# Self attention's output product on a two-layer Perceiver kernel: one full-precision product against three one-pass products of split operands

## The reference

```python
x = x + _L0_xattn_ref(_layernorm(x, axis=-1), ctx_512, ...)
x = x + _L0_attn_ref(_layernorm(x, axis=-1), ...)
x = x + _L0_ffn_ref(_layernorm(x, axis=-1), ...)
x = x + _L1_xattn_ref(_layernorm(x, axis=-1), ctx_512, ...)
x = x + _L1_attn_ref(_layernorm(x, axis=-1), ...)
x = x + _L1_ffn_ref(_layernorm(x, axis=-1), ...)
```

## Time and profile before

| | us |
|---|---|
| median of 3 runs | 2112.19 |
| lowest and highest of them | 2111.12, 2112.30 |
| span of the profiled execution, first to last instruction | 2106.8 |
| PE busy in it | 1996.1 (95%) |
| DVE, POOL, ACT busy | 1203.5 (57%), 972.1 (46%), 898.1 (43%) |
| L0a's first to last output product on PE | 440.4 to 532.6 |
| L1a's first to last output product on PE | 1462.3 to 1561.0 |

### The profile page before, as it was taken

The page is one execution under the profiler, slowest core; times in us unless marked ns, Lnnn a source line. Parts: engine busy times, 40 slices in busy tenths (PEclk is TensorE's granted clock), DMA queues, the critical chain, the costliest instruction groups (busy, mean ns, idle before and its releaser), DMA issues. The chain is left out here.

```text
span 2106.8 us, 28714 instructions
## 1 busy us (share of the span) xinstructions
PE 1996.1 (95%) x9018; PEld 1421.9 (67%) x9018; DVE 1203.5 (57%) x2739; ACT 898.1 (43%) x2115; POOL 972.1 (46%) x928
## 2 busy tenths in 40 slices
PE   7989999998999999999998999979978999999997
PEld 6868888776688744666656888767655555555553
DVE  4368998567551022555547899779863443444444
ACT  2356666334422100333335666635524444454542
POOL 1266684211352100676768666476203444555552
PEclk9999999999999999999999999989988999999999
DMA  5421221200311100111222121110345999989887
GB/s 209 150 100 42 58 58 37 82 1 1 120 42 52 35 1 0 52 57 61 70 107 66 43 67 43 66 67 1 110 148 154 312 298 327 210 213 221 209 218 186
DMA packets 103411, 226.29 MB, mean 107 GB/s; under 512 B 14288, under 2 KB 56784, under 8 KB 94768
## 3 DMA queue, kind: packets, MB, share of 16 engines
q1 hardware_dynamic: 80688, 170.85, 24.0%
q0 software_dynamic: 21136, 51.11, 11.9%
q10 hardware_dynamic: 1440, 2.49, 0.3%
HBM read 266.86 MB, written 42.48 MB: 147 GB/s over the span
## 5 line engine op out<-in xcount | busy, mean ns | idle before, releaser
L98 PE MATMUL banks<-L1f_w,L1f_xT 128*128 x760 | 265.1, 492 | 1.9 <-issue 1.3
L2872 POOL DMA_INDIRECT moe_sums<-L1f_y,L1f_row x94 | 149.3, 1589 | 219.5 <-DVE L1f_is_who L2739 162.2
L159 POOL TENSOR_TENSOR rstd<-rstd,power 128x1 f32<-128x1 f32 x48 | 35.4, 738 | 361.1 <-DVE rstd L153 361.1
L98 PEld LDWEIGHTS banks<-L1f_w,L1f_xT 128*128 128x128 f32 x760 | 138.0, 192 | 82.0 <-issue 6.8
L2690 DVE SCALAR_TENSOR_TENSOR L1f_z<-banks,L1f_share,L1f_sg 128x192 f32<-128x192 f32 x95 | 39.7, 418 | 147.8 <-ACT L1f_sg L2623 147.7
L2880 POOL DMA_INDIRECT L1f_xg<-moe_rows,L1f_row x95 | 94.2, 991 | 61.5 <-DVE L1f_spare L2730 24.6
L2623 ACT ACTIVATE L1f_sg<-banks 128x192 f32<-128x192 f32 x95 | 31.4, 331 | 206.9 <-PE banks L98 145.5
L98 PE MATMUL banks<-L0f_down,L0f_z 128*128 128x512 f32 x256 | 111.1, 592 | 1.5 <-DVE L0f_z L2147 1.5
L98 PE MATMUL banks<-L0f_hT_hi,L0f_ug_hi 128*128 128x512 f32 x256 | 100.0, 391 | 0.0
L98 PE MATMUL banks<-L0f_hT_hi,L0f_ug_lo 128*128 128x512 f32 x256 | 99.6, 389 | 0.0
L98 PE MATMUL banks<-L0f_hT_lo,L0f_ug_hi 128*128 128x512 f32 x256 | 99.6, 389 | 0.0
(11 more groups left out here) (425 smaller groups left out, 5672.5 us busy)
## 6 DMA issues: line engine op xcount, KB each, us to landing
L1f_w<-in_experts SPq DMA_DIRECT2D x95, 1280.0 KB
L1f_laid<-moe_counts SPq DMA_DIRECT2D x59, 512.0 KB
w<-in_L1x_heads SPq DMA_DIRECT2D x16, 704.0 KB, 4.1
w<-in_L0x_heads SPq DMA_DIRECT2D x8, 1216.0 KB, 5.7
w<-in_wug SPq DMA_DIRECT2D x8, 1024.0 KB, 4.9
L0x_craw<-in_ctx SPq DMA_DIRECT2D x96, 64.0 KB, 2.9
L1x_craw<-in_ctx SPq DMA_DIRECT2D x96, 64.0 KB, 2.2
w<-in_L0x_out SPq DMA_DIRECT2D x4, 1280.0 KB, 5.5
```

Source lines behind the costliest of these rows:

```text
L98: ins = pe.e.matmul(out, w, m, start=first and n == 0, stop=last and n == len(pairs) - 1)
L159: pool.e.tensor_tensor(self.rstd[:, i:i + 1], self.rstd[:, i:i + 1], self.power[:, 0:1], ALU.pow).then_inc(self.rstd_set.sem, 1)
L2872: pool.e.indirect_dma_start(self.sums[j % 2][:, :], bass.IndirectOffsetOnAxis(ap=self.row[:, j:j + 1], axis=0), self.y[j % self.NY][:], No ...
```

## The change

In both self attentions the turned values are kept as a leading part `oT_hi` (float32r, ACT's copy as before) and a remaining part `oT_lo` (`values_lo`, a new subtraction on DVE, per tile, behind `mask_scores`, or in the end by hand behind the statistics). The weights are split once per attention: `output_hi`, a copy of 128x2048 on ACT at the end of its step 1, and a subtraction of 128x2048 on POOL in its step 2. `project_out` issues 12 one-pass products where it issued 4 full ones. In L0a the leading weights have a tile of their own; in L1a they and `oT_lo` lie in the slots of the k and v weights. To find the memory, tiles of L0f are laid out anew, `moved` gets its own place over `ug`, and the row `ws_down` is loaded later, by itself.

```diff
-        self.oTb = [sb(f"oTb{i}", [P, AT, P]) for i in range(2)]
+        self.oT_hi = [sb(f"oT_hi{i}", [P, AT, P], F32R) for i in range(2)]
...
             else:
                 pe.wait_ge(self.o_set, n + 1)
+                pe.wait_ge(self.o_lo, n + 1)
...
     def project_out(self, pe, i):
         self.bank7_free(pe, "output", i)
-        self.w[3].landed(pe)
+        pe.wait_ge(self.wo_hi, 1)
+        pe.wait_ge(self.wo_lo, 1)
         pe.wait_ge(self.o_set, i + 1)
-        accumulate(pe, self.sh.psum(7), [(self.oTb[i % 2][:, t, :], self.w_o[:, t, :])
-                                         for t in range(AT)]).then_inc(self.projected.sem, 1)
+        pe.wait_ge(self.o_lo, i + 1)
+        values = (self.oT_hi[i % 2][:], self.oT_lo[i % 2])
+        accumulate(pe, self.sh.psum(7), [p for t in range(AT) for p in parts(
+            cut(values, slice(None), t), cut(self.w_out, slice(None), t))]).then_inc(self.projected.sem, 1)
...
+            if i == 1:
+                self.output_hi(act)
...
+    def output_hi(self, act):
+        self.w[3].landed(act)
+        act.wait_ge(self.wk_lo, 1)
+        act.e.copy(self.w_out[0], self.w_o).then_inc(self.wo_hi.sem, 1)
...
+            if 0 <= i - 5 < NT:
+                self.values_lo(dve, i - 5)
             if 0 <= i - 2 < NT:
                 self.spread_dve(dve, i - 2)
...
         self.keep_mixed(dve, NT - 3)
         self.mask_scores(dve, NT - 1)
+        self.values_lo(dve, NT - 3)
         self.after.rows_early(dve, last)
         self.sum_weights(dve, NT - 1)
         self.keep_mixed(dve, NT - 2)
         self.add_output(dve, NT - 3)
+        self.values_lo(dve, NT - 2)
         self.after.rows_early(dve, last + 1)
         self.keep_mixed(dve, NT - 1)
         self.add_output(dve, NT - 2)
+        self.values_lo(dve, NT - 1)
         self.after.rows_early(dve, last + 2)
         self.add_output(dve, NT - 1)
...
+    def values_lo(self, dve, i):
+        hi, lo, bank = self.oT_hi[i % 2][:], self.oT_lo[i % 2], self.mix_bank("values", i)
+        dve.wait_ge(self.w_lo, 2)
+        dve.wait_ge(self.o_set, i + 1)
+        dve.wait_ge(self.projected, i - 1)
+        hi, lo = (v.rearrange("p t (s b) -> p t b s", s=S) for v in (hi, lo))
+        dve.e.tensor_tensor(lo, bank.rearrange("p (t b s) -> p t b s", t=AT, s=S), hi, ALU.subtract).then_inc(self.o_lo.sem, 1)
...
+            if i == 2:
+                pool.wait_ge(self.wo_hi, 1)
+                pool.e.tensor_tensor(self.w_out[1], self.w_o, self.w_out[0], ALU.subtract).then_inc(self.wo_lo.sem, 1)
...
-        for w in (*self.wd, *self.wug):
+        for n, w in enumerate((*self.wd, *self.wug)):
             w.load(sp)
+            if n == len(self.wd):
+                self.begin(sp)
+                sp.e.dma_start(self.ws_down[:], d["ws_down"].to_broadcast([P, D])).then_inc(self.ws_down_landed.sem, 16)
```

More of the change, by code:

```diff
@@ L117, in __init__ @@
         self.rstd = keep("rstd", [P, NT])
-        self.w = [keep(f"w{i}", [P, SLOT]) for i in range(NSLOT)]
+        with ExitStack() as part:
+            self.w = [part.enter_context(nc.sbuf_tensor(f"w{i}", [P, SLOT], F32)) for i in range(NSLOT)]
+        self.w_parts = [keep(f"w_part{i}", [P, SLOT], F32R) for i in range(NSLOT)]
         self.ident = keep("ident", [P, P])
@@ L1347, in __init__ @@
         self.p_turned, self.pT_set = take("p_turned", NT), take("pT_set", NT)
-        self.mixed, self.o_set = take("attn_mixed", NT), take("o_set", NT)
+        self.mixed, self.o_set, self.o_lo = take("attn_mixed", NT), take("o_set", NT), take("o_lo", NT)
+        self.wo_hi, self.wo_lo = take("wo_hi", 1), take("wo_lo", 1)
         self.projected, self.x_added = take("attn_projected", NT), take("attn_x", NT)
@@ L1363, in __init__, with part_of @@
             ("wv", vw, [(self.w_hi, 3), (self.w_lo, 2)]), ("wo", D, [(self.projected, NT)]))]
+        def part_of(n, a):
+            return sh.w_parts[self.w[n].k % NSLOT][:, a:a + KD * D].rearrange("p (k n) -> p k n", k=KD)
         self.w_o = self.w[3].ap[:, 0:KD * D].rearrange("p (k n) -> p k n", k=KD)
+        if normed:
+            self.w_out = (part_of(1, 0), part_of(3, 0))
+            self.oT_lo = [sh.w_parts[self.w[2].k % NSLOT][:, n * D:(n + 1) * D].rearrange("p (t n) -> p t n", t=AT) for n in range(2)]
+        else:
+            self.w_out = (sb("wo_hi", [P, KD, D], F32R)[:], part_of(3, 0))
+            self.oT_lo = [sb(f"oT_lo{i}", [P, AT, P], F32R)[:] for i in range(2)]
         self.bank7 = []
@@ L1915, in __init__ @@
         self.other = self.z[:, FC // 2:FC, :].rearrange("p a n -> p (a n)").rearrange("p (a n) -> p a n", a=FC)
+        self.ws_down = sb("ws_down", [P, D])
+        with ExitStack() as part:
+            self.moved = part.enter_context(sh.nc.sbuf_tensor(f"{name}_moved", [P, D], F32))[:]
+        self.ug = [tuple(sb(f"ug_{v}{i}", [P, KD * P], F32R) for v in ("hi", "lo")) for i in range(3)]
         self.had = sb("had", [P, 2, P])
@@ L1918, in __init__ @@
         self.ws_up, self.ws_gate = sb("ws_up", [P, FC]), sb("ws_gate", [P, FC])
-        self.ws_down, self.su = sb("ws_down", [P, D]), sb("su", [P, FC])
-        self.ug = [tuple(sb(f"ug_{v}{i}", [P, KD * P], F32R) for v in ("hi", "lo")) for i in range(3)]
+        self.su = sb("su", [P, FC])
         self.sg = [sb(f"sg{i}", [P, TOK]) for i in range(2)]
@@ L1926, in __init__ @@
         self.half = sb("half", [P, KD, P])
-        self.moved = self.half[:].rearrange("p k n -> p (k n)")
         self.stages = [(self.down[:], self.other, 1), (self.other, self.down[:], 2), (self.down[:], self.other, 4),
                        (self.other, self.down[:], 8)]
-        self.tabs = take("ffn_tabs", 16 * 6)
+        self.tabs, self.ws_down_landed = take("ffn_tabs", 16 * 5), take("ws_down_landed", 16)
         self.scaled = take("ffn_scaled", 1)
@@ L2094, in scalar @@
                 self.keep_rows(act, NT - 2 + q)
-        act.wait_ge(self.tabs, 16 * 6)
+        act.wait_ge(self.tabs, 16 * 5)
         act.wait_ge(self.hx_lo, NT)
@@ L2160, in scale_rows @@
         scale = self.su_ug[:].rearrange("p (k o) -> p k o", o=1).to_broadcast([P, KD, P])
[L2161 removed]
+        dve.wait_ge(self.tabs, 16 * 5)
         self.turned(dve, i)
```

4 lines of the change are left out of this document (2 added, 2 removed).

## The result

| | us |
|---|---|
| before, median of 4 runs | 2112.18 |
| changed, median of 4 runs (lowest and highest) | 2124.94 (2124.31, 2125.72) |
| changed / before, with its 95% interval | 1.0059 [1.0047, 1.0071] |
| span of the profiled execution | 2122.5, its own time 2124.31 |

A forecast was written before the change was run, and what follows sets the result against it. PE, busy 95%, was taken as the bound, with DVE's list as long in some steps. Terms +1.7 (L0a), +0.8, +4.2 (L1a) and +0.3 (clock) gave +7.0: 2112.2 to 2119.2 us, range 2108.5 to 2123.

The forecast's parts named there:

- (c): Added cost of loading `ws_down` for L0f: one DMA issue on SP long before its use, nothing.
- Steps: L0a, steps 5 to 9: PE's shorter output products against DVE's added subtractions, sum -0.2 us.
- End: End of L0a: tile 7's remaining part comes behind tile 6's statistics and delays the last output product, +1.9 us.
- it isn't caught up: End of L0a: the +1.8 us delay stays, since PE already waits for DVE's `xn` at the chain's end.
- Cheap reordering: Rival: DVE's subtraction takes 0.69 us in both attentions; +1.3 us in all, 2113.5; chance 0.27.
- The block: L1a, step 2: POOL's 128x2048 weight subtraction holds up DVE's two-operand SBUF row, PE waits for `xn`; +4.2 us.
- The clock: L1a, behind PE's new stall: PE's clock runs low; bounds nothing and 3.5 us, taken as +0.3.
- The steps and the end: L1a, steps 5 to 9 and end: DVE's subtraction delays PE, less -0.7 us in the end part; sum +0.8.
- Forecast: The main case: +7.0 us, 2119.2 us, own range 2116 to 2122; chance 0.38.
- long low clock: Rival: the low clock behind L1a's stall costs 3.5 us more than the main case, 2122.7; chance 0.10.
- slower: The outcome of a kernel measurably slower than before, with the bound at 2116.4 us; chance 0.50.

The follow-up runs named there:

- e1: The kernel before with only L0f's part of the change (`ug` 1312 bytes lower, `ws_down` and `moved` changed); 2118.12 us, ratio 1.0032.
- e2: The changed kernel with L0f's `ug` back at its old byte, small tables moved behind `half`; 2121.34 us, ratio 1.0047.
- e3: The changed kernel with L0f's `ug` 32 bytes higher, at a multiple of 64; median 2123.07 us, six runs from 2115.88 to 2128.45.
- e9: The kernel before with `ug` moved by 32 bytes, off a multiple of 64, `sg` and `hT` kept in place; 2117.44 us, ratio 1.0030.
- e12: The kernel before with `ug`, `sg`, `hT` and `half` all moved up by 32 bytes; one run, 2112.23 us.
- e13: The kernel before with only `hT` and `half` moved up by 32 bytes, `ug` kept in place; one run, 2117.56 us.
- e14: The changed kernel with tile 7's `values_lo` taken between tile 6's addition to x and its statistics, in both attentions; one run, 2126.88 us.
- e4: The changed kernel with `values_lo` walking by position, writing `oT_lo` straight on and reading PSUM in jumps; 2125.34 us.
- e5: The changed kernel with both `values_lo` and ACT's `keep_values` walking by position; 2117.59 us, ratio 1.0030.
- e6: The changed kernel with L1a's output weight subtraction moved from POOL in step 2 to DVE in step 1; 2122.71 us, ratio 1.0051.
- e7: The changed kernel with `project_out` making the 8 products of leading values before it waits for `oT_lo`; 2126.16 us, ratio 1.0067.
- e8: The changed kernel with `ug` 32 bytes higher, `values_lo` and `keep_values` by position, L1a's weight subtraction on DVE; 2108.41 us, ratio 0.9981.
- e0: The kernel before, unchanged, as a control; 2110.4 us.

## Why the prediction was wrong

**The sum.** +7.0 were predicted, and the attentions do add 1.7 + 5.3 = 7.0, in part by luck (see below). The rest is L0f, and the step that failed is (c). The prediction costed the third part of the change by "the loading of `ws_down` costs one DMA issue on SP long before its use: nothing"; that is right for the DMA, but the same lines move `ug` by 1312 bytes, which is 20 times 64 and 32 more, and the prediction went past that without costing it. What stood at nothing measures 5.1 us. No rival had it either, so the range left out a stage in which nothing is computed differently. e1, e2 and e3 show it, e9, e12 and e13 what it depends on.

**L0a.** Steps: -0.2 predicted, -0.1 found from the first `on` to tile 7's (+0.22 up to tile 4, then -0.33). End: +1.9 predicted, +1.84 found, and that is luck. The term was a start 2.5 later and a product 0.7 shorter. Found are a start 1.1 later after `on`, a product 1.7 longer at the clock of 0.50, which wasn't in the term, and 1.0 made up behind it, which was ruled out ("it isn't caught up"). The start is late by less because the 1.2 by which tile 6's remaining part was to move DVE's list don't appear: the statistics start 0.8 earlier after L0a's first `on` than before, not 0.7 later. That fits tile 6's product being shorter, for whose end DVE waited 0.56 ahead of `add_output` before and doesn't wait now. The place behind the statistics does cost, as e14 shows, but most of it by way of the clock.

**`values_lo`.** 1.17 us was taken from ACT's copy; 1.04 to 1.11 measured. It is the jumps in SBUF that cost, for ACT's copy those of its write: e4 and e5 bring DVE's and ACT's rows to 0.69 and 0.59 with the jumps on the PSUM side. The Trainium skill's rule (SBUF — State Buffer, the box on cachelines under "Door 1: The DMA port swizzle") that an access which goes to a new 16-byte line pays agrees in kind with these 1.04 to 1.11 and 1.08 us. "Cheap reordering" was a real possibility, only not in this code.

**L1a.** The block: 4.2 predicted. The start of `xn` on DVE ahead of the block is 10.33 later than in the profile before, that of the next, behind it, 14.46: 4.1. The clock: 0.3 predicted, out of bounds of 0 to 3.5; PE is at 0.71, 0.50 and 0.94 in the 6 us behind the stall, and the next `xn` is another 1.3 late. I had argued that DVE's list goes on regardless; in fact DVE then waits 1.41 us for the slower PE's scores. So block and clock come to 5.4, and e6 takes out 5.6. Against the mean of the unchanged attentions the stage is 5.8 longer up to tile 0's `on`; 4.5 were predicted. The steps and the end: +0.8 predicted, -0.6 found: +1.1 up to tile 3's `on` (PE waits 2.10 us where it waited 1.17), and -1.7 behind it, where -0.7 was thought. The errors cancel: 5.3 predicted, 5.3 found, and that too is luck.

**Chances.** Forecast and long low clock together had 0.48, and slower 0.50. The side was right. The size is wrong by the term of L0f; without it the attentions alone would have come out at the forecast, but with the clock mis-sized at both places where PE stalls and the end of L1a mis-sized against it.

## What to carry to other kernels

When a change lays tiles out anew, treat every stage whose tiles move as changed, and compare the rate of its products in equal windows; a slower rate has no wait to show it. When a stage has several bounds close together (here PE, DVE's list and ACT's copy), cost the stalls too by what the clock does behind them: e4 and e7 gave back in low stretches of their traces the 2.1 and 2.8 us that they had gained in L1a, while e5 and e8, which gained more, came out in the time. When a term comes out right, look whether its parts do: here L0a's end and L1a fitted in sum and not in their parts. An operation that reorders should jump on the PSUM side and write SBUF straight on, and a long POOL subtraction belongs where DVE has nothing to do, or on DVE itself: 2.28 us in an idle hole, beside POOL's power and unhindered by it (e6), against 4.1 us of standstill.

## What was unexpected of the hardware

**The place of one operand relative to the other.** One-pass products of 128x512 start 0.2267 us apart if the tile of the weights that PE loads and the tile that streams through lie to each other as before or 1280 bytes from that, and 0.2333 (2.9% more) if 32 bytes, either way, or 1312 from that, in L0f, where PE runs 768 of them without a pause. Shifts by 64 or by less than 32 bytes weren't tried. In the other stages the products run 0.2267 (L1a's with `wk` and `wv`) to 0.232 apart in either layout; why some are slower stays open, and whether the relation matters there wasn't tried.

**The clock falls after like waits in one execution and not in another.** The same kernel, the same row (PE, L1f's gate, after 0.76 us of waiting), windows of 3 us in the profile before:

```profile
1529.00:1532.00 3.00, 3.00 (x45) 2.96 (x46) 0.06 (x1) 0.00 (x0) 0.55 (x1) 1.00 0.43 154
1532.00:1535.00 3.00, 3.00 (x40) 2.80 (x38) 1.68 (x3) 0.44 (x1) 0.00 (x0) 1.00 0.00 0
```

and in e0:

```profile
1529.00:1532.00 3.00, 3.00 (x30) 2.76 (x31) 0.18 (x2) 0.00 (x0) 0.55 (x1) 0.72 0.47 171
1532.00:1535.00 3.00, 3.00 (x42) 2.74 (x40) 0.69 (x1) 0.00 (x0) 0.00 (x0) 0.71 0.00 1
```

e0 loses 1.6 us there. Such places stand at 400 to 407, 506 to 516, 848 to 861, 1435 to 1446 and 1522 to 1550 in one trace or another. With the start (PE's rows near 38 us differ by 3 us) they are what I find in the traces for the spread of the runs, the widest of which is e3's, 12.6 us; as each kernel has one trace, how much of the spread they make isn't shown.
